# A fused attention and feed-forward kernel: moved start-up and weight transfers, a new order in the third unit, and a unit's two halves of each product made together on alternating banks

## The reference, cut to what matters

```python
def sparsify_2to4(h):                 # of each 4 neighbours the 2 largest |h| stay
    _, idx = jax.lax.top_k(jnp.abs(h.reshape(..., 4)), 2)
    ...
def ffn(x, w_gate, w_up, w_down):
    h = jax.nn.silu(jnp.einsum('bsh,hi->bsi', x, w_gate)) * jnp.einsum('bsh,hi->bsi', x, w_up)
    return jnp.einsum('bsi,ih->bsh', sparsify_2to4(h), w_down)

x = x + tanh(g_xattn) * attention(layernorm(x), ctx, mask)     # keys and values are both ctx
x = x + tanh(g_ffn) * ffn(layernorm(x), w_gate, w_up, w_down)
```

## Time and profile before

| | |
|---|---|
| runs (median; lowest and highest of 3) | 1100.33 us; 1098.69, 1100.50 |
| profiled execution: its time; its span | 1101.53 us; 1099.7 us |
| busy: PE, DVE, ACT, POOL | 98%, 72%, 56%, 21% of the span |
| granted TensorE clock, mean | 0.998 |
| DMA | 254.75 MB, mean 232 GB/s |
| chain that ended last: PE, DVE, DMA, issue | 72%, 13%, 5%, 4% |

### The profile page before, as it was taken

How to read it: one execution, slowest core, us unless ns; L and a number is a source line. 1 busy time by engine, 2 the same in 40 slices (tenths; PEclk the granted TensorE clock), 3 DMA queues, 4 the chain that set the end, 5 groups by cost and what they waited for, 6 DMA issues and landing times.

```text
span 1099.7 us, 15140 instructions
## 1 busy us (share of the span) xinstructions
PE 1074.9 (98%) x4960; PEld 879.4 (80%) x4960; DVE 797.0 (72%) x1391; ACT 611.6 (56%) x1124; POOL 225.7 (21%) x342
## 2 busy tenths in 40 slices
PE   7998899999999999999999999999999999999998
PEld 6876677788888788888888888888888888888886
DVE  5999879898997667675766666676757565665775
ACT  6998676786864444454545544454544444443452
POOL 6887511122211111001111111100011111111101
PEclk9999999999999999999999999999999999999999
DMA  8998694899969977797859877797879666767726
GB/s 289 362 358 294 211 400 145 246 307 293 305 193 367 286 202 201 200 278 197 232 141 367 223 185 184 187 276 202 237 207 329 153 156 155 192 152 189 200 29 134
DMA packets 89965, 254.75 MB, mean 232 GB/s; under 512 B 9120, under 2 KB 9632, under 8 KB 85536
## 3 DMA queue, kind: packets, MB, share of 16 engines
q1 hardware_dynamic: 68288, 205.55, 52.6%
q0 software_dynamic: 21600, 48.24, 25.9%
HBM read 154.14 MB, written 99.61 MB: 231 GB/s over the span
## 4 chain that ended last, share of the span: by engine, by line
PE 72%; DVE 13%; DMA 5%; issue 4%; SPq 2%; ACT 2%; POOL 1%; DVEq 0%; ACTq 0%; POOLq 0%
PE ps_y L1332 10%; PE ps_y L1334 9%; PE ps_y L1333 9%; PE ps_a L1261 9%; PE ps_a L1263 8%; PE ps_a L1265 8%; PE ps_d L1265 4%; PE ps_d L1261 4%; PE ps_d L1263 4%; PE ps_c L1261 2%; PE ps_c L1265 2%; PE ps_c L1263 2%; DMA x_blk<-xnT_scratch 2%; DVE x L959 2%; DMA x_in<-in_x 2%
## 5 line engine op out<-in xcount | busy, mean ns | idle before, releaser
L598 POOL DMA_DIRECT2D out_rows<-y_out x124 | 105.7, 855 | 735.8 <-ACT y_out L743 732.2
L1261 PE MATMUL ps_a<-xm,w_ring 128*128 128x512 f32 x512 | 200.2, 391 | 1.9 <-DMA xm<-xm_scratch 0.8
L1263 PE MATMUL ps_a<-xm,w_ring 128*128 128x512 f32 x512 | 199.6, 390 | 0.0
L1265 PE MATMUL ps_a<-xm,w_ring 128*128 128x512 f32 x512 | 199.5, 390 | 0.0
L1332 PE MATMUL ps_y<-dn,h_hi 128*128 128x512 f32 x480 | 188.9, 394 | 3.2 <-ACT y_out L743 2.9
L1334 PE MATMUL ps_y<-dn,h_lo 128*128 128x512 f32 x480 | 187.9, 392 | 0.0
L1333 PE MATMUL ps_y<-dn,h_hi 128*128 128x512 f32 x480 | 187.3, 390 | 0.0
L743 ACT ACTIVATE y_out<-ps_y,ffn_gate 128x512 f32<-128x512 f32 x124 | 85.1, 687 | 177.4 <-PE ps_y L1334 177.3
L720 ACT ACTIVATE h_hi<-hidden 128x512 fp32r<-128x512 f32 x128 | 73.2, 626 | 84.6 <-DVE hidden L1031 84.4
L1005 DVE TENSOR_TENSOR beats<-h_abs 128x512 bf16<-128x512 f32 x186 | 117.7, 684 | 1.4 <-ACT h_abs L713 1.3
L1261 PEld LDWEIGHTS ps_a<-xm,w_ring 128*128 128x128 f32 x512 | 96.1, 188 | 24.3 <-issue 1.4
(11 more groups left out here) (114 smaller groups left out, 1874.4 us busy)
## 6 DMA issues: line engine op xcount, KB each, us to landing
w_ring<-w_scratch SPq DMA_DIRECT2D x147, 512.0 KB, 4.4
out_rows<-y_out POOLq DMA_DIRECT2D x124, 256.0 KB, 4.2
w_scratch<-w_ring SPq DMA_DIRECT2D x56, 512.0 KB, 5.6
xm_scratch<-x_out SPq DMA_DIRECT2D x42, 512.0 KB, 5.4
xm<-xm_scratch SPq DMA_DIRECT2D x21, 1024.0 KB, 11.6
w_raw<-in_L_ffn_w_down SPq DMA_DIRECT2D x9, 1024.0 KB, 7.5
x_in<-in_x SPq DMA_DIRECT2D x32, 256.0 KB, 5.3
ctx_in<-in_ctx SPq DMA_DIRECT2D x32, 256.0 KB, 5.5
```

Of the source, the lines that this page charges most:

```text
L598: nc.gpsimd.dma_start(out[RING * (n // (2 * TILES * QS)) + TILES * ORDER[order] + n % TILES], y_out[:, n % 4], accum_op=ALU.add).then_inc( ...
L1261: nc.tensor.matmul(to, w_ring[:, k, e, 0, c], xm[:, k, 0, c], start=begins and c == 0, stop=False, skip_group_check=not begins)
L1263: nc.tensor.matmul(to, w_ring[:, k, e, 0, c], xm[:, k, 1, c], start=False, stop=False, skip_group_check=not begins)
L1265: last = nc.tensor.matmul(to, w_ring[:, k, e, 1, c], xm[:, k, 0, c], start=False, stop=c == 1, skip_group_check=not begins)
```

## The change

In the order of the diff: (1) the pieces (1, 2) and (1, 3) are loaded in slots 28 and 29, not 22 and 23, and unit 0's operands are stored in slots 30 to 36, not one slot after each is made; (2) at the start SP issues the gates' and masks' loads some samples later and the first two weight pieces after samples 6 and 7 in place of both after 5; (3) at a pair's change SP's `x_stored_at` stands inside the loop over the seven xm loads, not ahead of it; (4) ACT makes the tanh of the gates in slot 3 ahead of probsT, not at the end of slot 2; (5) in step 1 ACT copies y of tiles 0 and 1 ahead of two h_high and two silu; (6) in the last seven slots DVE does `bn_aggr` after x1n and `x_sum` after x1; (7) in step 1 DVE's `x_low_at` comes after the units' w_sum and w_low, not ahead of `count_wins`; (8) PE's `product(u, k, e)` becomes `products(u, k)`: the waits of both e first, then 12 matmuls in which e alternates fastest.

```diff
--- before.py
+++ after.py
@@ -56,9 +56,10 @@
 ORDER = (1, 0)
 
 
-PIECE_AT = {6: (0, 2), 7: (0, 3), 11: (1, 0), 12: (1, 1), 22: (1, 2), 23: (1, 3), 38: (2, 0)}
+PIECE_AT = {6: (0, 2), 7: (0, 3), 11: (1, 0), 12: (1, 1), 28: (1, 2), 29: (1, 3), 38: (2, 0)}
 SPREAD_AT = {5: ((0, 0),), 6: ((0, 1),), 10: ((0, 2),), 11: ((0, 3),), 21: ((1, 0),), 22: ((1, 1),), 37: ((1, 2), (1, 3))}
 SUM_AT = {12: (0, 0), 13: (0, 1), 14: (0, 2), 15: (0, 3)}
+STORE0_AT = {30 + k: k for k in range(PROD)}
 W0_AT = {7: 0, 8: 1, 15: 2, 16: 3, 17: 4, 18: 5, 19: 6}
 X0_AT = {22 + i: (0, i) for i in range(7)} | {29 + i: (1, i) for i in range(7)}
 
@@ -437,16 +438,16 @@
 
             for b in range(INPUTS):
                 load(b)
-                if b == 5:
-                    load_w_piece(sp, nc.sync, 0, 0)
-                    load_w_piece(sp, nc.sync, 0, 1)
-                if b in (3, 4):
-                    load_mask(b - 2)
                 if b == 2:
                     load_mask(0)
+                if b == 4:
                     for n, g in enumerate((g_xattn, g_ffn)):
                         sp.dma_start(gates_in[:, n:n + 1], g.rearrange("(a n) -> a n", a=1)
                                      .to_broadcast([P, 1])).then_inc(gates_loaded, 16)
+                if b in (4, 5):
+                    load_mask(b - 3)
+                if b in (6, 7):
+                    load_w_piece(sp, nc.sync, 0, b - 6)
             load_mask(3)
             for n in range(SLOTS):
                 if 0 <= n - 5 < B:
@@ -462,8 +463,8 @@
                                  ).then_inc(xnT_stored[h % 2], 16)
                 if n in PIECE_AT:
                     load_w_piece(sp, nc.sync, *PIECE_AT[n])
-                if n - 1 in W0_AT:
-                    store_w(0, W0_AT[n - 1])
+                if n in STORE0_AT:
+                    store_w(0, STORE0_AT[n])
                 if n == SLOTS - 3:
                     load_x_blk(sp, 1, 0)
 
@@ -494,16 +495,16 @@
                         if half == 1:
                             x_stored_at(s, 3)
                     else:
-                        if u + 1 not in RELOADED:
-                            x_stored_at(s, 2)
                         for k in range(PROD):
                             if u + 1 in RELOADED:
                                 load_w(u + 1, k)
                                 if k == 3:
                                     x_stored_at(s, 2 * half)
                             elif u + 1 < UNITS:
+                                if s < QS and k == 2:
+                                    x_stored_at(s, 2)
                                 if k == PROD - 1:
-                                    x_stored_at(s, 3)
+                                    x_stored_at(s, 3 if s < QS else 2)
                                 load_xm(p + 1, k)
                                 if k == 3 and p in range(1, PAIRS - 2):
                                     load_x_blk(sp, p + 2, 0)
@@ -665,16 +666,16 @@
                     last.then_inc(nT_copied, 1)
                 b = n - 3
                 if 0 <= b < B:
+                    if b == 0:
+                        act.wait_ge(gates_loaded, 32)
+                        nc.scalar.activation(xattn_gate[:], gates_in[:, 0:1], ACT.Tanh).then_inc(gates_done, 1)
+                        nc.scalar.activation(ffn_gate[:], gates_in[:, 1:2], ACT.Tanh).then_inc(gates_done, 1)
                     act.wait_ge(pT_done, b + 1)
                     wait(act, av_done, b - 1)
                     if b == 0:
                         act.wait_ge(gates_done, 1)
                     nc.scalar.activation(probsT[:, b % 2], ps_pT[:, 0:P], ACT.Identity,
                                          scale=xattn_gate[:]).then_inc(pT_copied, 1)
-                if n == 2:
-                    act.wait_ge(gates_loaded, 32)
-                    nc.scalar.activation(xattn_gate[:], gates_in[:, 0:1], ACT.Tanh).then_inc(gates_done, 1)
-                    nc.scalar.activation(ffn_gate[:], gates_in[:, 1:2], ACT.Tanh).then_inc(gates_done, 1)
                 if n in W0_AT:
                     w_high(act, 0, W0_AT[n])
                 if n in X0_AT:
@@ -797,12 +798,14 @@
                         spread(act, u + 1, 3)
                     if s <= QS:
                         copy_y(s - 1, 0, 0)
+                    if s == 1:
+                        copy_y(s - 1, 0, 1)
                     for j in tiles[:2]:
                         h_high(s - 1, 1, j)
                     silu1(u, 0)
                     silu1(u, 1)
                     for t in range(TILES):
-                        if s > QS or t > 0:
+                        if t > (1 if s == 1 else 0 if s <= QS else -1):
                             copy_y(s - 1, 0, t)
                         if building:
                             for k in ((), (2, 3), (4, 5), (6,))[t]:
@@ -917,12 +920,16 @@
 
         @block.vector
         def _(dve):
+            def aggregate(n):
+                b = n - 6
+                if 0 <= b < B:
+                    dve.wait_ge(bn2_done, b + 1)
+                    nc.vector.bn_aggr(stats[:, n % RING, 1], bn6[:, 1, b % 2]).then_inc(stats2_done, 1)
+
             dve.wait_ge(stats_set, 1)
             for n in range(-2, SLOTS):
-                b = n - 6
-                if 0 <= b < B:
-                    dve.wait_ge(bn2_done, b + 1)
-                    nc.vector.bn_aggr(stats[:, n % RING, 1], bn6[:, 1, b % 2]).then_inc(stats2_done, 1)
+                if n < B:
+                    aggregate(n)
                 b = n + 1
                 if 0 <= b < B:
                     dve.wait_ge(bn1_done, b + 1)
@@ -933,6 +940,8 @@
                     dve.wait_ge(power_done, n + 1)
                     nc.vector.tensor_scalar(x1n[:, b % 2], x1[:, b % 4], stats[:, (n - 1) % RING, 1, 0:1],
                                             power3[:, (n - 1) % RING, 1:2], ALU.subtract, ALU.mult).then_inc(x1n_done, 1)
+                if n >= B:
+                    aggregate(n)
                 b = n - 3
                 if 0 <= b < B:
                     wait(dve, probs_done, b - 1)
@@ -949,7 +958,7 @@
                 if n == SLOTS - 1:
                     w_sum(dve, 1, 0)
                     w_sum(dve, 1, 1)
-                if n in X0_AT:
+                if n in X0_AT and n < B:
                     x_sum(dve, 0, *X0_AT[n])
                 b = n - 5
                 if 0 <= b < B:
@@ -958,6 +967,8 @@
                     wait(dve, x1_stored[b % 4], 16 * (b // 4))
                     nc.vector.scalar_tensor_tensor(x1[:, b % 4], ps_av[b % 2][:], power3[:, (n - 1) % RING, 2:3],
                                                    x_in[:, b % INPUTS], ALU.mult, ALU.add).then_inc(x1_done, 1)
+                if n in X0_AT and n >= B:
+                    x_sum(dve, 0, *X0_AT[n])
                 b = n - 5
                 if 0 <= b < B:
                     dve.wait_ge(x1_done, b + 1)
@@ -1089,7 +1100,6 @@
                     compare(0, 1, REST)
                     add_c12(u, 0)
                     add_c12(u, 1)
-                    x_low_at(s, 0)
                     count_wins(0, 1)
                     keep(0, 1, tiles[:2])
                     for j in tiles[:2]:
@@ -1106,6 +1116,8 @@
                             w_sum(dve, u + 1, i)
                         for k in range(2, 4):
                             w_low(dve, nc.vector, u + 1, k)
+                    if s == 1:
+                        x_low_at(s, 0)
                     if s >= QS:
                         x_low_at(s, 1)
                 else:
@@ -1224,7 +1236,7 @@
 
             bank = (ps_a, ps_c, ps_a, ps_d, ps_a, ps_d, ps_a)
 
-            def product(u, k, e):
+            def ready(u, k, e):
                 p = u // (2 * QS)
                 if e == 0:
                     if u < BUILT:
@@ -1255,16 +1267,19 @@
                     pe.wait_ge(d0_copied[e], u + 1)
                 if k == 6:
                     pe.wait_ge(c22_done[e], u + 1)
-                to = bank[k][e][:]
+
+            def products(u, k):
+                for e in range(2):
+                    ready(u, k, e)
                 begins = k in (0, 1, 3)
                 for c in range(2):
-                    nc.tensor.matmul(to, w_ring[:, k, e, 0, c], xm[:, k, 0, c], start=begins and c == 0, stop=False,
-                                     skip_group_check=not begins)
-                    nc.tensor.matmul(to, w_ring[:, k, e, 0, c], xm[:, k, 1, c], start=False, stop=False,
-                                     skip_group_check=not begins)
-                    last = nc.tensor.matmul(to, w_ring[:, k, e, 1, c], xm[:, k, 0, c], start=False, stop=c == 1,
-                                            skip_group_check=not begins)
-                last.then_inc(made[k], 1)
+                    for left, right in ((0, 0), (0, 1), (1, 0)):
+                        for e in range(2):
+                            last = nc.tensor.matmul(bank[k][e][:], w_ring[:, k, e, left, c], xm[:, k, right, c],
```

(17 more changed lines are left out.)

## The result

The changed kernel takes 1113.83 us (median of 4 runs, 1113.41 to 1114.36) against 1100.41 us for the kernel before (4 runs): a ratio of 1.0111, 95% interval 1.0091 to 1.0130. It is slower, as forecast, but by 13.4 us, not by 2.8, and outside the range (1095.0 to 1106.2). The profiled execution took 1114.01 us (span 1112.2), 12.5 more than that of before.

What follows compares the result with a forecast made beforehand. TensorE (PE), busy 98% of the span, was taken as the bound. Terms -5.7 + 1.7 + 3.2 + 2.2 + 0.4 + 1.0 = +2.8 us gave 1103.1 us on the median; range 1095.0 to 1106.2.

Steps and rivals of the forecast that it cites:

- rival (c): Feed-forward matmuls: alternating banks shorten the pitch; 3 ns less gives 1095.0 us; chance 0.07.
- rival (d): Feed-forward matmuls: cycling banks leave idle times and the clock falls; +54 us, 1154; chance 0.02.
- moved `x_stored_at`: SP's queue at a pair's change: costs 0, at most 1.08 us a pair.
- removed wait on y_out: Before unit 3: moved copy_y removes a 2.94 us wait and 1.7 us of slow clock, freeing PE by 4.6.
- new waits in units 1 and 2: PE's k0 waits for e=1's gates at both unit changes: +2.0, then another 1.1, together +3.1 us.
- units 0 to 3: Units where weights are still built: +1.7 us in all, bounds -4.6 and +4.8.
- x_in waits: Attention stage: DVE's waits for x_in shrink, -1.7 us at start-up and -3.8 with unit 0's stores moved.
- the reordering: Last seven slots: bn_aggr and x_sum behind x1n and x1 leave the chain of x1, -0.2 us.
- Rival (e): Attention stage: x_in stays late because of the xnT stores, so the -3.8 is lost: 1106.9 us; chance 0.04.
- Units 4 to 31 and the end: Units 4 to 7 +3.2, six units with dn_low +2.2, units 12 and 20 +0.4, end +1.0 us.
- Rival (a): Units 1 to 7 and later: delays overlap, only 3.7 of 7.5 us shows: 1099.3 us; chance 0.25.
- rival (b): PE keeps the 5.7 and part of the 4.6 us stall, paying few new waits: 1096.2 us; chance 0.17.

Runs made afterwards that it cites:

- experiment 1: Two runs: changed kernel with `x_stored_at` back ahead of the xm loads, 1107.80 us; kernel before with only `x_stored_at` moved, 1107.03 us.
- P alone: Kernel before with only the paired, alternating products: 1113.69 us, ratio 1.0101.
- X alone: Kernel before with only `x_stored_at` moved into the loop over the xm loads: 1107.03 us, ratio 1.0058.
- X undone: Changed kernel with `x_stored_at` back ahead of the seven xm loads: 1107.80 us, ratio 1.0056.
- DVE's order back: Changed kernel with DVE's `bn_aggr` and `x_sum` of the last seven slots where they stood: 1112.02 us, ratio 1.0083.
- experiment 6: Kernel before with only ACT's copy_y of tile 1 moved ahead in step 1: 1101.97 us, ratio 1.0005.

## Why the prediction was wrong

**The bound and the pitch: right.** PE bounds the kernel, the alternation changes nothing in the pitch (0.2270 against 0.2271), so rival (c) is out. The lower clock came with waits of PE of 1.85 us and more, never from the alternation itself, as rival (d) had it: between 380 and 900 us the matmuls of every product of the changed kernel alternate, and the granted clock is 1.00:

```profile
380.00:640.00 260.00, 258.22 (x1135) 212.35 (x1134) 169.64 (x280) 123.98 (x220) 30.58 (x36) 1.00 0.82 225
640.00:900.00 260.00, 259.52 (x1139) 213.26 (x1138) 170.46 (x284) 119.13 (x211) 28.91 (x34) 1.00 0.79 214
```

So what the section "A second HAM failure mode: psum-queue depth-cycling" of the Trainium skill's "TensorE: Matmul & The Clock Gate" reports of another kernel doesn't show in this one. (A slip in the working: by the unrounded rows the two pitches differ by 0.15 ns, so a change of bank gives -1.8 ns, not -2.4. The value taken was 0 in any case. And the DMA engines give more than the 390 GB/s called the most: slices of the same trace between 310 and 385 us reach 428.)

**The step that failed: SP.** The prediction costed the moved `x_stored_at` at 0 and at most 1.08 us, with the words that the waits "have nothing behind them that is near its need". Behind the moved one stood five of the seven xm loads, the last of which PE waited for already in the kernel before (0.82 us at 366.84, experiment 1). That row named the need; the prediction took its bound from another wait instead. Nor did it ask what the store now goes out behind: its landing took 10.8 us instead of 5.5. The term cost 6.0 us in the changed kernel and 5.9 alone, 45% of the loss. It doesn't account for the whole miss: without it the changed kernel takes 1107.80 us, still 1.6 above the range. The two misses that follow, 1.6 and 1.4 us, make the rest.

**Waits costed without the clock behind them.** The prediction credited the removed wait on y_out with 1.7 us of clock, but charged its own new waits in units 1 and 2 for their length only. The lengths were right (+2.1 and +1.1 against 2.0 and 1.1); behind the second the clock fell and cost 1.6 us more, which is as much as the whole miss in units 0 to 3 (+3.3 against +1.7). That this miss isn't larger is luck in part: behind the 1.85 at 141.03 and the 1.93 at 202.60 the clock could have fallen as well. With P alone it fell at both unit changes (+1.5, +1.6).

**The start.** The x_in waits went as forecast: at the residual of sample 26 the changed kernel is 6.2 us ahead (102.13 against 108.32), against 5.7 forecast. By the first feed-forward matmul it is 4.3 ahead. 2.1 us went into two x_sum that met POOL's x_low; the prediction had called the reordering a gain of 0.2 and had not looked at what POOL does at that moment. Rival (e), stores moved without effect, is out.

**Units 4 to 31 and the end: right.** +3.4, +2.3 and +1.0 against +3.2, +2.2 and +1.0, from the slack of e=1's source at each hand-over. Units 12 and 20 cost 0.9 against 0.4; since X alone costs 0.9 in unit 12 too, most of that seems to belong to X; how X does it was not followed. Rival (a), that the delays overlap and only half of them shows, is out; rival (b), the stall's gain kept, is out too: copy_y alone gains nothing that can be measured.

## What to carry to other kernels

Before moving an entry in an in-order DMA queue, list every entry that it moves ahead of and behind, and ask for the last one's consumer: a store behind two large loads lands later (10.8 us against 5.5 here), a wait for its landing inside a row of loads shifts all that follow, and a consumer that already waits a little (0.8 us here) pays for it in full. Making two products as a pair is free only where the second buffer has its whole lead to spare and nobody waits for the first product; elsewhere each hand-over costs, and a wait of some 2 us may cost nearly as much again in clock. And a part that moves time forward (the start-up loads here) earns it only if nothing later waits for something that doesn't move with it.

## What the runs showed that was not expected

- Two-input VectorE instructions on SBUF and POOL's wait for each other: 0.68 us becomes 1.51 or 1.75, 1.26 becomes 1.82, according to who starts first. Residuals, which read one operand from PSUM, and statistics, which read one operand, kept their 0.74 and 0.70 us beside the same POOL instruction. One operand isn't the rule, though: x1n reads one large operand too and took 0.90 us instead of 0.53 when it started inside it (106.41, POOL 105.33 to 107.02).
- The fall of the clock isn't a fixed price of a wait. At the unit changes, behind 1.85 us of waiting, it fell in five of eight cases (changed kernel one of two, X undone one of two, DVE's order back one of two, P alone two of two), at 1.5 to 1.6 us each; behind the 2.34 of experiment 6 it didn't. In the profiled executions, from 100 us on, it fell with each of seven waits of 2.89 us and more, in 14 of 23 of 1.85 to 2.34, and behind none of 1.2 to 1.6.
- The same store of 512 KB landed after 5.5 us ahead of two 1 MB loads and after 10.8 behind them; the next one after 10.3 or 14.2 us, according to how long before it four such loads had been issued.
